# W2's last quarter and b1's second half load behind the fourth gather; two quarters of x are issued from ScalarE's queue

## What is computed

```python
x = x + 0.5 * ffn(layernorm(x))      # the expert of a row is the argmax of x @ gate_w.T + gate_b + expert_bias
x = x + attn(layernorm(x), context)  # softmax over all 512 keys, sharpened by 1.5
x = x + 0.5 * ffn(layernorm(x))
# ffn, for the rows of expert e:  relu(x @ w1[e] + b1[e]) @ w2[e] + b2[e]
```

## Time and profile before

| | |
|---|---|
| Median of 3 runs | 744.68 us (744.66 to 745.38) |
| The profiled execution | 745.16 us, span 743.4 us, mean granted clock 0.988 |
| Busy in the span | PE 96%, DVE 81%, PEld 80%, ACT 67%, POOL 49% |
| The chain that ended last | PE 71%, DVE 13%, DMA 6%, issue 5%, POOL 3% |

### The profile page before, as it was taken

How to read it: one execution, slowest core, us unless ns; L and a number is a source line. 1 busy time by engine, 2 the same in 40 slices (tenths; PEclk the granted TensorE clock), 3 DMA queues, 4 the chain that set the end, 5 groups by cost and what they waited for, 6 DMA issues and landing times.

```text
span 743.4 us, 15250 instructions
## 1 busy us (share of the span) xinstructions
PE 711.4 (96%) x4374; PEld 597.0 (80%) x4374; DVE 602.4 (81%) x1645; ACT 497.0 (67%) x1212; POOL 367.4 (49%) x499
## 2 busy tenths in 40 slices
PE   9989999899999999999999999999999999989992
PEld 7769888788888888878878878887887887769991
DVE  6989999887788887888788788787878778788892
ACT  3677777677677677667667767766766676546661
POOL 5067887243343454345346345434534633586662
PEclk9999999999999999999999999999999999999996
DMA  9942432200000000000000000000000011232210
GB/s 248 346 144 47 97 86 71 60 19 1 2 0 1 2 8 8 2 4 12 0 1 15 2 1 11 5 0 4 13 1 1 16 44 64 94 91 64 55 47 5
DMA packets 31792, 31.49 MB, mean 42 GB/s; under 512 B 5049, under 2 KB 26183, under 8 KB 31200
## 3 DMA queue, kind: packets, MB, share of 16 engines
q1 hardware_dynamic: 27360, 23.91, 10.9%
q0 software_dynamic: 3520, 6.40, 3.2%
q10 hardware_dynamic: 832, 0.21, 0.1%
HBM read 20.96 MB, written 10.47 MB: 42 GB/s over the span
## 4 chain that ended last, share of the span: by engine, by line
PE 71%; DVE 13%; DMA 6%; issue 5%; POOL 3%; ACT 0%; another core or an unknown queue 0%; SPq 0%; DVEq 0%; POOLq 0%; ACTq 0%
PE bank L1478 16%; PE bank L1480 15%; PE bank L1479 15%; PE bank L1691 13%; PE bank L1527 4%; DMA x_packed<-slot_rows 3%; DVE neg_max L1363 2%; PE bank L1513 2%; DVE probsT_lo L1369 2%; DMA slot_rows<-x_stats,row_of_slot 2%; PE bank L1530 1%; DVE hT_lo L1219 1%; DMA rows<-in_L_attn_x 1%; POOL rows L585 1%; PE bank L1732 1%
## 5 line engine op out<-in xcount | busy, mean ns | idle before, releaser
L601 POOL TENSOR_SCALAR probs<-probs,row_inv 128x512 f32<-128x512 f32 x256 | 178.2, 697 | 274.0 <-DVE row_inv L1374 263.1
L814 ACT ACTIVATE probs<-bank,neg_max 128x512 f32<-128x512 f32 x256 | 176.4, 689 | 143.9 <-DVE neg_max L1363 142.8
L1363 DVE TENSOR_REDUCE neg_max<-bank 128x1 f32<-128x512 f32 x256 | 176.5, 689 | 86.7 <-PE bank L1480 83.5
L1369 DVE TENSOR_TENSOR probsT_lo<-bank,probsT_hi 128x512 fp32r<-128x512 f32 x256 | 174.2, 680 | 2.2 <-ACT probsT_hi L823 2.0
L1691 PEld LDWEIGHTS bank<-ident,probs 128*128 128x128 f32 x1024 | 127.1, 140 | 38.7 <-issue 2.0
L1691 PE MATMUL bank<-ident,probs 128*128 128x128 f32 x1024 | 153.5, 272 | 1.7 <-POOL probs L601 1.2
L823 ACT ACTIVATE probsT_hi<-bank 128x512 fp32r<-128x512 f32 x256 | 151.2, 591 | 2.1 <-PE bank L1691 2.1
L1478 PE MATMUL bank<-m_hi,xT_hi 128*128 128x512 f32 x256 | 122.4, 478 | 0.0
L1478 PE MATMUL bank<-probsT_hi,vw_hi 128*128 128x512 f32 x256 | 101.7, 397 | 3.5 <-DVE probsT_lo L1369 3.5
L1479 PE MATMUL bank<-probsT_lo,vw_hi 128*128 128x512 f32 x256 | 101.5, 396 | 0.0
L1480 PE MATMUL bank<-probsT_hi,vw_lo 128*128 128x512 f32 x256 | 101.4, 396 | 0.0
(11 more groups left out here) (221 smaller groups left out, 1244.2 us busy)
## 6 DMA issues: line engine op xcount, KB each, us to landing
b<-in_L_ffn_b SPq DMA_DIRECT2D x4, 1024.0 KB, 9.0
x_packed<-slot_rows SPq DMA_DIRECT2D x39, 65.5 KB
slot_rows<-slots SPq DMA_DIRECT2D x39, 65.5 KB
x_stats<-rows SPq DMA_DIRECT2D x4, 524.0 KB, 10.2
rows<-x_packed SPq DMA_DIRECT2D x8, 262.0 KB, 3.0
rows<-in_L_attn_x SPq DMA_DIRECT2D x4, 512.0 KB, 8.3
w_lo<-in_L_ffn_w SPq DMA_DIRECT2D x8, 256.0 KB, 7.0
w_hi_lo<-in_L_ffn_w SPq DMA_DIRECT2D x8, 256.0 KB, 8.7
```

Of the source, the lines that this page charges most:

```text
L601: pool.tensor_scalar(PR[:, u % 4, :], PR[:, u % 4, :], RI[:, u % 4:u % 4 + 1], 1.0, ALU.mult, ALU.mult).then_inc(normed, 1)
L814: act.activation(PR[:, n % 4, :], BK[n % 2][:, :], ACT.Exp, bias=NM[:, n % 4:n % 4 + 1], accum_out=SU[:, n % 4:n % 4 + 1]).then_inc(probs, 1)
L1363: v.tensor_reduce(NM[:, n % 4:n % 4 + 1], BK[n % 2][:, :], AX.X, ALU.max, negate=True)\
L1369: v.tensor_tensor(PTL[at], BK[2 + u % 2][:, :].rearrange("p (c q) -> p c q", c=KC), PTH[at].bitcast(fp32), ALU.subtract).then_inc(pT_lo, 1)
```

## The change

The second and the fourth quarter of x are issued by ACT, behind gate_w and behind expert_bias. The second wait of SP's program goes from the gather of tile 1 to that of tile 3. The high parts of w2 for the experts 6 and 7 are taken one step later, in steps 4 and 5. LEAD is 8 in place of 7. Nothing else differs.

```diff
-        W2_HIGHS = {0: [2], 1: [3, 4], 2: [5], 3: [6], 4: [7]}
+        W2_HIGHS = {0: [2], 1: [3, 4], 2: [5], 4: [6], 5: [7]}

+        def load_x(eng, c):
+            eng.dma_start(ROWS[:, CH * c:CH * c + CH, 0:D], x_rows[:, CH * c:CH * c + CH, :]).then_inc(x_in[c], 16)
+
         @block.sync
         def _(sp):
-            def load_x(c):
-                sp.dma_start(ROWS[:, CH * c:CH * c + CH, 0:D], x_rows[:, CH * c:CH * c + CH, :]).then_inc(x_in[c], 16)
-
@@
-            for c in range(NCH):
-                load_x(c)
+            for c in range(0, NCH, 2):
+                load_x(sp, c)
             load_heads(0)
@@
             load_b2(0)
-            sp.wait_ge(pool_moved[1], 16)
+            sp.wait_ge(pool_moved[3], 16)
             load_w2(2)
             load_b1(1)
@@
-            LEAD = 7
+            LEAD = 8
             for j in range(LEAD):
                 gather(j)
@@
             act.dma_start(GWR[:, :], gate_w).then_inc(gate_in, 16)
+            load_x(act, 1)
             act.dma_start(GB[:, :], gate_b.partition_broadcast(P)).then_inc(small_in, 16)
             act.dma_start(EB[:, :], expert_bias.partition_broadcast(P)).then_inc(small_in, 16)
+            load_x(act, 3)
             act.dma_start(CTX[:, :, :], context.rearrange("b m c -> (b m) c").rearrange("(k p) c -> p k c", p=P))\
```

## The result

The changed kernel takes 753.81 us (median of 9 runs, 751.51 to 755.98); the kernel before, in the runs beside it, 745.38 (9 runs). The ratio is 1.0111, 95% interval 1.0091 to 1.0132: **slower by 8.3 us**, 6.8 to 9.8. The forecast was 742.3 in a range from 740.9 to 744.9. The profiled execution took 754.08 us, its span is 752.3.

A forecast was written before the change was run, and what follows sets the result against it. PE was taken to bound the kernel from 60 us on, so only earlier work and gaps up to 141 us could move. +0.2 -1.5 +0.2 -1.3 = -2.4 us from 745.16, less 0.5 for the median: 742.3, range 740.9 to 744.9.

The forecast's parts named there:

- The transfers are the same 2 MB: Start, 0 to 36 us: moving two x quarters to ACT's queue shifts two issues and leaves the bytes transferred unchanged.
- +0.2 us: Start, 0 to 36 us: net cost of the moved x loads, DVE's 0.71 us saving lost again; ends -0.7 and +2.2.
- The context follows with 0.46: Start, ACT's queue: the context's load is issued after the second held quarter, taking 0.46 us, before table and first copy.
- The hold: Start, ACT: its second x quarter is held until 5.7 us, so the first copy starts near 7.7 instead of 6.02.
- ACT is held and the clock falls: Rival, start: PE idles about 1.7 us and its clock falls, 2.2 us instead of 0.2, giving 744.3; chance 0.14.
- The slower rival: Start: second x quarter lands behind the third, 2.6 us later, clock falls; 4.3 us instead of 0.2, 746.4; chance 0.08.
- The gather: 36 to 57 us: with SP's loads behind it, tile 3's gather lands near 45.0 and ACT's wait goes; -1.5 us.
- LEAD: 57 to 141 us: gathers issued one turn earlier, ACT's waits down from 5.9 to under 2 us; -1.3 us.
- the forecast 2.6: 36 to 141 us: the gain summed for the later parts, gather, shared loads and LEAD together.
- 0.2 for shared loads: 36 to 57 us: gathers of tiles 5 to 7 share the queue with the moved loads; +0.2 us.
- The moved wait: Rival, 50 to 54 us: the late gather moves to tile 4, losing the 1.5 us again, 743.8; chance 0.14.
- the stores: Rival, from 57 us: POOL waits for stores instead, so LEAD gives nothing, 743.6; chance 0.07.

The follow-up runs named there:

- e2: All of the change except the x loads, which SP issues as in the kernel before: 744.05 us, ratio 0.9993 to the kernel before.
- e5: Changed kernel with SP's queue held before the heads until the second quarter of x has landed: 748.99 us, ratio 1.0098 to the kernel before.
- e12: Kernel before with only SP's wait moved to tile 3's gather and two high parts of w2 a step later: 741.63 us, ratio 0.9993.
- e13: Kernel before with LEAD 8 and nothing else: 740.19 us, ratio 0.9995 to the kernel before.
- e15: All of the change except the x loads, the kernel of e2 run again: 739.94 us, ratio 0.9973 to the kernel before.
- e7: Changed kernel with 40 more filler matmuls on PE, 10 ahead of later gates, 30 ahead of the context wait: 746.36 us, ratio 1.0075 to the kernel before.
- e6: Changed kernel with only SP's w1 loads held until the fourth quarter of x has landed: 747.98 us, ratio 1.0055 to the kernel before.
- e4: Changed kernel with the fourth quarter of x back on SP's queue, only the second on ScalarE's: 743.92 us, ratio 0.9995 to the kernel before.
- e3: Changed kernel with ScalarE issuing the context ahead of the fourth quarter of x: 753.55 us, ratio 1.0119 to the kernel before.

## Why the prediction was wrong

**The step that failed is "The transfers are the same 2 MB", and the +0.2 us built on it.** The part measured +9.5 alone. Three things went wrong in it.

- *What is pulled forward.* Two issues taken out of SP's queue let all behind them move up: SP's first heads are issued at 1.86 instead of 6.8, and w1 from 5.21 instead of 10.7 (the issues of e2, where SP loads x as before). With both held back the last quarter landed at 11.4 (e5), with them ahead at 16.0. The prediction counted the two loads on the queue that they came to, and not what the queue that they left would do with the room. It had the share rule at hand, and used it only for the gathers.
- *The context.* "The context follows with 0.46" priced its issue, and nowhere its landing. It took its turn behind a quarter of x, in the slower half of the share, and landed at 19.69; PE, in program order, had the gates of the last three eighths behind it.
- *The hold.* ScalarE was held, as the prediction said, but one issue later: the load behind two quarters was held, the context's (1.96 us), and not the second of the two (0.46). The first copy came at 7.10 instead of the forecast 7.7. The mechanism was right, and it had a rival of its own, "ACT is held and the clock falls", at 744.3. **Its price was the mis-sized term:** a fall was counted as 1.7 us, from 0.21 of 8 us in the earlier trace rows. Here the clock, once down, stayed down for 10 to 24 us, and the placing of e5 is 10.2 us late, its time 7.3. In the changed kernel's own profile it fell only at the wait for the context, so the rival's idle time was there and its fall came by another wait; the clock's part of the loss is 4.7 us.

*The slower rival*, the second quarter behind the third, did not happen: DVE took it at 7.80. That the loss would come from elsewhere in the same part, at 0.08, was far too little: the part had one priced resource (issue time) and two unpriced ones (the DMA engines' turns, the clock).

*The gather.* Right in the mechanism: in e2 no wait over 1 us for tile 3's gather, and clock 1.00 from 52 to 60. Its size is not confirmed: -1.5 was read off an engine's idle time at 49 us, and e12 gives 0.5 us, anywhere from 2.2 faster to 1.2 slower.

*LEAD.* The waits for gathers went as forecast, from 5.9 us to none in the view. Their removal alone gave 0.4 us (e13), which can't be told from nothing nor, with an interval to 1.8 us faster, from the forecast 1.3. With the gather the two gave 1 us, at most about 1.9, and not the forecast 2.6 (with the 0.2 for shared loads): this sum was too large.

*The moved wait* did not come back at tile 4, and the stores did not bind: POOL's waits for them after 60 us are 0.7 us in all in the changed kernel, 2.4 in e2 and 0.3 in e15, under the 3 that the prediction named.

## What to carry to other kernels

A load moved to another queue must be costed twice: what it waits for where it goes, and what the queue that it leaves now issues earlier; small pieces lose against large ones in the share. Before an engine's issue list is lengthened, look at what its first compute instruction releases: in e5 1.4 us of idle TensorE there cost five times that, since the clock fell. A row of filler matmuls in a known idle stretch is a cheap test, and sometimes a cure, as long as it ends before the data come; in e7's profile it didn't.

## What the runs showed that was not expected

- **A fall of the clock lasts much longer at the start than in the middle.** At 52 us it was 0.79 over 8 us. In the front PE ran at 1.2 GHz for 13.6 to 23.9 us in seven profiled executions, and for 10.2 us in e7, where ten filler matmuls (17.0 to 19.4) stood shortly ahead of the return at 20.0. Why it lasts so long stays open. The Trainium skill (TensorE: Matmul & The Clock Gate, section "What's actually happening") says that "activity releases the throttle". That the clock comes back at all agrees (0.99 from 32 to 44 us in e5); that it took through two stretches in which PE is busy 12.00 of 12.00 us by the profile is not what a reader would take from it.
- **The same kernel does both.** e6 fell in 8 of 12 runs and not in 4, 6 to 10 us apart, with the same instructions. The changed kernel kept its clock behind 1.46 us of idle time in its profile, e5 lost it behind 1.40. So whether such a stretch drops the clock can't be told ahead from its length.
- **Equal packets, not equal bytes**, between two queues with work: 1068 and 1066 in 6 us.
- **The load behind two quarters is the one held.** ScalarE's issue of the context took 1.8 to 2.9 us behind two quarters of x and 0.46 behind one (e4, and 0.48 in e3), while the second of the two quarters itself took 0.4 to 0.6; with gate_b behind the context, that was held too (2.18).
